# A graph layer's edge gathers wait for their own rows in mid-step, and ScalarE's step opens with root and attention

## The reference

```
xn  = layernorm(x)                                  # 6250 x 256
h   = (xn @ W).reshape(N, 4, 64)                    # graph attention, 4 heads
e   = leaky_relu(a_src[src] + a_dst[dst], 0.2)      # one per edge: 200,000 sorted by dst, and 6250 loops
p   = exp(e - segment_max(e, dst)[dst])
gnn = relu(segment_sum(p / segment_sum(p, dst)[dst] * h[src], dst) + bias)
mix = ...                                           # linear attention over all nodes, a gelu layer
x1  = x + gnn + mix
out = x1 + ffn(layernorm(x1))                       # 8 experts, the top two of each node, gelu
```

## Time and profile before

| | us |
|---|---|
| three timed runs | 2638.74, 2645.68, 2659.38 |
| median | 2645.68 |
| the profiled execution | 2648.4 |
| its span on the core | 2646.7 |

### The profile page before, as it was taken

One profiled execution on the slowest core, in us unless ns is written; L12 is line 12 of the kernel. 1 busy time (PEld: TensorE's weight loads), 2 busy tenths in 40 slices (PEclk: granted clock), 3 DMA queues, 4 the chain that ended last, 5 costly groups with the idle time before them and its releaser, 6 DMA issues. The chain is left out here.

```text
span 2646.7 us, 37526 instructions
## 1 busy us (share of the span) xinstructions
PE 1985.1 (75%) x9074; PEld 1410.8 (53%) x9075; DVE 1609.6 (61%) x3942; ACT 1081.6 (41%) x1932; POOL 1455.6 (55%) x1586
## 2 busy tenths in 40 slices
PE   8588888676767777667777888878788978888653
PEld 6356656455555555445455555555555656654332
DVE  7566666556666765586656656856665768642123
ACT  5322222234444444353544545555535555533110
POOL 3465655666666666655455555555566556520265
PEclk9789998887777777778889889989999988999887
DMA  9644444765555555544455555545556665521365
GB/s 324 138 137 131 133 127 112 236 175 149 149 151 153 152 155 144 151 132 143 142 171 163 140 157 154 153 137 146 154 146 173 163 166 154 149 83 56 114 195 161
DMA packets 286939, 401.66 MB, mean 152 GB/s; under 512 B 108851, under 2 KB 209491, under 8 KB 283198
## 3 DMA queue, kind: packets, MB, share of 16 engines
q0 software_dynamic: 74208, 206.08, 28.8%
q1 hardware_dynamic: 194348, 169.01, 21.9%
q10 hardware_dynamic: 18162, 24.08, 3.0%
HBM read 345.85 MB, written 81.96 MB: 162 GB/s over the span
## 5 line engine op out<-in xcount | busy, mean ns | idle before, releaser
L1529 POOL DMA_INDIRECT rows_g<-node_table,src_all x1347 | 1283.6, 953 | 927.9 <-issue 389.3
L2316 PE MATMUL psB<-rows_g,pick_e 128*128 128x260 f32 x2704 | 785.7, 451 | 125.1 <-issue 107.1
L2316 PEld LDWEIGHTS psB<-rows_g,pick_e 128*128 128x128 f32 x2704 | 603.9, 230 | 266.7 <-issue 155.4
L2115 ACT ACTIVATE pick_n<-local_row 128x1024 bf16<-128x1024 bf16 x169 | 178.6, 1057 | 505.8 <-remote 362.8
L1704 DVE TENSOR_TENSOR rows_g<-rows_g,psD 128x2048 f32<-128x2048 f32 x169 | 384.9, 2277 | 0.0
L2393 PE MATMUL psD<-W_f,hidT 128*128 x896 | 277.4, 463 | 0.0
L1767 DVE COPY xn<-psD 128x256 f32<-128x256 f32 x112 | 47.4, 423 | 336.7 <-PE psD L2393 107.9
L2357 PE MATMUL psC<-W_f,xnT 128*128 x448 | 227.0, 629 | 0.0
L2393 PEld LDWEIGHTS psD<-W_f,hidT 128*128 128x128 f32 x896 | 195.9, 230 | 46.7 <-issue 6.5
L1551 POOL DMA_INDIRECT rows_g<-set_dram,places x98 | 96.5, 984 | 202.8 <-issue 176.5
L2111 ACT ACTIVATE local_row<-local_row,minus_id 128x1024 bf16<-128x1024 bf16 x169 | 191.6, 1134 | 34.3 <-issue 20.9
(11 more groups left out here) (386 smaller groups left out, 2982.8 us busy)
## 6 DMA issues: line engine op xcount, KB each, us to landing
local_row<-local_dram SPq DMA_DIRECT2D x169, 256.0 KB
rows_g<-node_table,src_all POOLq DMA_INDIRECT x1347
xin<-sent_dram SPq DMA_DIRECT2D x112, 128.0 KB
set_dram<-xn SPq DMA_DIRECT2D x112, 128.0 KB
xnT<-in_xT_dram SPq DMA_DIRECT2D x96, 128.0 KB
sent_dram<-sorted_dram SPq DMA_DIRECT2D x96, 128.0 KB
sent_dram<-sorted_dram ACTq DMA_DIRECT2D x96, 128.0 KB
acc<-node_table SPq DMA_DIRECT2D x49, 128.0 KB
```

What stands on the lines that cost most here:

```text
L1529: pool.indirect_dma_start(out=rows_g[:, r, j], out_offset=None, in_=node_table, in_offset=bass.IndirectOffsetOnAxis(ap=src_all[:, g, j:j + ...
L2115: act.activation(pick_n[:], local_row[:, r], ACT.Relu, bias=1.0, scale=-1.0).then_inc(pick_n_ready, 1)
L2316: last = pe.matmul(ps_sum[s % 2][:, 0:AW], pick_e[:, s % SLOTS, j], rows_g[:, s % RING, j, 0:AW], start=(j == 0), stop=(j == EG - 1))
```

## The change

Two edits. In POOL's gather, the wait ahead of the fifth transfer asks for the count that the slot's semaphore has when the step's own first four transfers have landed (four times 16 above the earlier uses of the slot), and no longer for `picked`. In ScalarE's loop root and attention stand at the front of the step, ahead of the spot choices and the picks; the instructions are the same.

```
                         if j == EG // 2 and s >= 1:
-                            pool.wait_ge(picked, s)
+                            pool.wait_ge(gathered[r], 16 * (EG * (s // RING) + EG // 2 - (EG - LAST_COLS if r == 0 else 0)))
                             pool.sem_inc(pool_gate, 1)
...
                     for s in range(STEPS):
+                        for t in range(FULL, -1, -1):
+                            if route_at[t] + 2 == s:
+                                root(t)
+                            if route_at[t] + 1 == s:
+                                attention(t)
                         if 2 <= s < PAIRS + 2:
                             kv_deviations(s - 2)
...
                             take_h(*jobs_with(s - 2))
-                        for t in range(FULL, -1, -1):
-                            if route_at[t] + 2 == s:
-                                root(t)
-                            if route_at[t] + 1 == s:
-                                attention(t)
                         if jobs_with(s - 1):
                             gelu(*jobs_with(s - 1))
```

## The result

The changed kernel is slower, by about 1%. Its median is 2669.34 us (2665.92 to 2681.10, 11 runs) against 2647.39 us of the kernel before beside it (2638.74 to 2659.38, 11 runs), 22 us more. The recorded ratio of the runs is 1.0095, with a 95% interval from 1.0073 to 1.0117, which is 25 us. 2609 us was forecast, with a range up to 2655.

The account below looks back on a forecast made before the run. No engine is full, so waits set the time, chiefly PE's posts held by unbroken gathers. Stage terms -9 + 2 - 24 - 8 = -39 us, with 0 for the reorder, took 2648.4 to 2609 us; 8-in-10 range 2575 to 2655.

Parts of the forecast that it names:

- PE's posts are held while gathers run unbroken: POOL's gathers: while they follow without a pause, PE's semaphore posts arrive late, after the run drains; picks waited 121.7 us early.
- POOL becomes the bound: Rival: POOL drains in every step; at a 3.3 us drain its floor is 13.0 us, +28 us, 2676 us; chance 0.17.
- A: First 41 steps of the gather loop, 12.55 us a step: -9 us, limited by POOL's floor.
- B: Next 37 steps of the gather loop, the stage with the scatters, 14.04 us a step: +2 us.
- D: 23 steps of the gather loop after C, 12.70 us a step, already near POOL's floor: 0 taken.
- C: 46 steps of the gather loop after B, 14.04 us a step: -24 us, the floor's bound being 79 us.
- I take 2.6 us and a floor of 12.32 us: POOL's mid-step wait: drain of 2.6 us, floor of 12.32 us a step, 14.93 us with two scatters.
- What a shorter run saves: Near 2250 us: posts would come at 2252.90 instead of 2257.36, about 0.6 of the wait; applied to 39.9 us: -24 us.
- E: Last 20 steps of the gather loop, 13.05 us a step: -8 us, half of the 15 the floor allows.
- slower case: The rival POOL becomes the bound: drain in every step, break-even at a drain of 3.0 us, 2676 us; chance 0.17.

Follow-up runs that it names:

- both waits: Kernel before, with the fifth gather waiting for PE's previous pick and also for the step's own first four gathers; ScalarE as before: ratio 1.0067.
- a stop every other step: Kernel before, with the new wait for the first four gathers in odd steps only and no mid-step wait in the others: ratio 1.0453.
- three in flight: Kernel before, with no stop in mid-step; each gather waits for the landing of the one three ahead of it: ratio 1.0158.

## Where the prediction was right and where it was wrong

**Right.** That PE's posts are held while gathers run unbroken. The prediction read it from two places; the trace of the kernel before lets it be counted, with a run of gathers and scatters ended by 0.8 us without one, and a post late when it comes more than 1 us after its pick. The posts of 154 of the 169 picks have a record. Of 51 picks that end while POOL stands still 2 posts are late; of 40 that end in the first four gathers of a run, 8; of 63 that end in the fifth or later, all, 4.4 us at the median. Of the 73 late posts 56 come 0.8 to 3.2 us after the end of the last gather, the others while gathers still run. It is no rule: in the changed kernel 67 of 81 posts are late in the fifth gather or later, and the 14 that are not all lie in steps 0 to 42. Right also that the gathered rows were never late before, and that the reorder is worth nothing that can be measured: 0 was taken, 0.22% (-0.01 to 0.46) measured.

The rival named "POOL becomes the bound", priced at 2676 us, came nearest to the 2669 measured, and its cause is the one that the runs show in A and B. That its sum is so near is partly luck: it had A at +18, B at +27, D at +7 and C still at -24, and measured were +14, +13, +4 and -6. The Trainium skill's rule that spoke against the edit ("DMA: Bandwidth & Descriptors", Rules for kernel authors: issue early, wait late) had the right sign; the trace agrees, with 478.4 us of stops on POOL. But the kernel that follows that rule furthest, with no wait in mid-step, was 3.5% slower, so the measurement decides against it as a guide for this wait.

**Wrong: stages A and B.** The step that failed is "I take 2.6 us and a floor of 12.32 us". The 2.6 us were those of the old wait, which ends with a post of PE; the new one ends when four gathers have landed, and that is longer in every stage: 3.20 us in A, 2.77 in B, 2.96 in C, and 2.92 in D, where the 2.6 were read (after, 1820 to 2115.6 us):

```profile
POOL rows_g L1529 <- DMA rows_g<-node_table,src_all: 64.3, 22, 4.0
```

So A's -9 became +14 and B's +2 became +13. In A a difference of 0.6 us in one wait, 41 times, is 25 us, which covers the miss of 23; in B 0.17 us in 37 steps is 6 of the 11 missed, and the other 5, by which the stage runs above POOL's floor, have no row. The prediction itself had held A's gain down by the floor; with the floor within 2% of the pace, the range of the drain should have set the sign, not its mean.

**Wrong: stage C.** The step that failed is "What a shorter run saves", -24 us where -6 was measured. It took runs of four for granted. The row that it was read from is a run of eight gathers of one step, and the prediction cut that run in half. With the new wait the second half of a step and the first half of the next join, eight again, as long as the head of a step finds its slot free. In steps 80 to 125 POOL stopped at the head of a step 26 times before and 12 times after; the runs were 65 of 5.7 gathers on the mean before and are 61 of 6.0 after. And it overlooked what the old wait did in this stage (before, 1158 to 1804 us):

```profile
POOL rows_g L1529 <- PE psA L2305: 113.3, 26, 9.9
...
POOL rows_g L1529 <- remote: 65.0, 26, 3.3
```

In 26 of 46 steps POOL stood still until PE's pick itself had ended, and a pick that ends while POOL stands still has a prompt post. Of the picks of these steps whose post has a record 24 of 45 ended so before, 6 of 43 after; in the fifth gather of a run or later ended 11 before, 19 after, and all of these posts were late. Held picks rose from 39.9 to 58.4 us. The kernels with half of the change agree: 23 of 46 picks ended with POOL at rest with the reorder alone, 8 of 42 with POOL's wait alone. But with both waits, where the pause for the pick remains, the picks of stage C still wait 62.5 us for held posts; how much of the missing 18 us is due to joined runs and how much to the lost pause is not shown. E's -8 became -1 and D's 0 became +4, and kernels with the same wait differ by about as much in these stages.

**Wrong: the weights.** The slower case had a chance of 0.17 and its unknown, the drain, was known to reach from a mean of 2.59 to 3.9 us, with the break-even at 3.0. Such a chance should follow from how much of the unknown's span lies on either side of the break-even.

**As forecast among the signs to look for:** the picks' held waits fell to less than half in A and B, not in C; no run of gathers was longer than eight; DVE's waits for rows rose from 10.2 us to 164.6, the sign of the rival; B stayed under 14.5, and A went above 12.8. Not as forecast: POOL's stop, 3.01 us on the mean and not 2.5 to 2.7, and stage C, 13.92 us a step and not 13.5. For root and attention DVE waits 16.0 us by name after (6.9 and 9.1), against 119.7 (71.8 and 47.9); the largest case of before became this:

```profile
1755.54 10.21 ACTq L2173 DMA_DIRECT2D sent_dram<-sorted_dram  x4
...
1765.78 1.28 ACT L2152 ACT_TABLE_LOAD   x1 [11.24 <-DMA sent_dram<-sorted_dram]
...
1767.40 0.16 DVE L1800 RECIPROCAL rr<-std_r 128x1 f32<-128x1 f32 x1 [3.55 <-issue]
```

The root stands right behind the four transfers (the first row's 10.21 us) and DVE follows at once, having waited 3.55 us and not 14.62. What it saved brought no gain that can be measured: the reorder alone is at 1.0022.

**Open.** Why a stop every other step is worse than none, and by what way a post is held while gathers are issued. No run here separates POOL's issuing from the transfers in flight, as three in flight lay between the two expectations. PE itself can be slow in such a stretch: the 16 matmuls of the sum that starts at 596.90 us, beside the earlier trace rows, take 12.0 us, against 3.8 us at the median. And the length of the runs is not the whole of it: with no wait in mid-step no run in steps 80 to 125 is longer than eight either, and the stage takes 14.79 us a step.

## What to carry to other kernels

A wait that only paces an engine is worth what it does to the engines beside it; before it is replaced by one that is always late, ask in each stage what ends it now, add up the pacing engine's own step, stop included, with the stop's spread, and compare it with the present pace stage by stage. Where the floor comes within a few per cent of the pace, removed waits come back as waits for that engine. And when runs are to be cut, count what joins on the other side of the cut.

## What the hardware showed that I had not expected

Unbroken runs of indirect gathers on POOL go with late semaphore posts of PE: up to 12.88 us for one pick, and 4.2 us of ScalarE's waits for picks in all over 46 steps when no run was longer than four. Where in the run the matmul ends matters: in the kernel before, 63 of 63 posts were late from the fifth gather on, 2 of 51 with POOL at rest. A kernel whose gathers stop nowhere in mid-step was 3.5% slower for it. And a stop until four gathers of 128 rows have landed is not a constant: 2.60 us in the rows from 305 us on, 3.20 us on the mean of stage A, and 6.0 us at the longest there.
